# X kept centred in SBUF from the first stage on, the input's mean added back by a product in the last turning

## The chip, the cores and the metric

The kernel runs on one core of a Trainium2 chip. The metric is the device time of one execution in microseconds. Before the change it is 1280.5 us, the median of three runs (1279.04 to 1280.61).

## What is computed

Four residual blocks follow one another on x of shape (2, 2048, 128): time mixing with a channel-mixing gate, a ternary feed-forward net, a state-space scan, a mixture of experts. Each normalises its input and its output over the 128 channels:

```python
def _layernorm(x, axis=-1, eps=1e-05):
    m = jnp.mean(x, axis=axis, keepdims=True)
    v = jnp.var(x, axis=axis, keepdims=True)
    return (x - m) / jnp.sqrt(v + eps)
...
x = L0_attn_x
x = x + _layernorm(_L0_attn_ref(_layernorm(x), ...))   # 1 time mixing, with its own
...                                                    #   two norms and channel mixing
x = x + _layernorm(_L0_ffn_ref(_layernorm(x), ...))    # 2 ternary feed-forward
x = x + _layernorm(_L1_attn_ref(_layernorm(x), ...))   # 3 state-space scan
x = x + _layernorm(_L1_ffn_ref(_layernorm(x), ...))    # 4 mixture of experts
```

The scan of stage 3 runs over 2048 steps for 256 channels and 16 states, `state = dA * state + dBu`, with `y = sum(state * C)`, after a causal convolution of four taps. Stage 4 sends each token to two of eight experts.

Every addend of x is itself the output of a layernorm, so its mean over the channels is zero. The mean of x over the channels is the same in all four blocks: that of the input.

## The kernel before

X lies in SBUF as 128 channels (partitions) by 2 x 2048 tokens, fp32. Work goes in tiles of N = 512 tokens: NT = 4 tiles in time (t), B = 2 rows of the batch (b), so eight tiles of 128x512. A mean over channels is a mean over partitions, so it is made by TensorE: `G.centre` is the matrix I − 1/128, which gives x minus its mean in a PSUM bank, and `G.ones` holds 1/128 throughout, which gives the mean of squares after ScalarE's square. fp32 products of 128x512 appear in the profile as two instructions.

In each block a tile is first centred by such a product (`centre`, `centre_B`, `next_centre_B`, `prep` step 0, `next_stage` step 0), squared by ScalarE out of the bank, averaged by the ones product, turned into 1/sqrt by a logarithm and an exponential on ScalarE, and multiplied from the bank by VectorE.

The program is four functions with a barrier between each: `phase_time_mix` (0 to 150 us), `phase_ffn` (150 to 470), `phase_ssm` (470 to 976), `phase_moe` (976 to 1279). Each engine has its own instruction list, written out by hand in the order of execution; semaphores join them. A wait stands in its engine's list and holds everything behind it.

- `phase_time_mix`: PE's `centre(t)` writes banks C[0], C[1]; `square` and `inverse_roots` are ScalarE's, `normalise` (L615, L616) is VectorE's. At its end the first tile of stage 2 is prepared (`next_centre_B`, L361; `next_square_B`, L504; `next_normalise`, L734). Names: tiles in the order P2_ORDER = (1, 2, 0, 3) in stage 2.
- `phase_ffn`: PE runs through fp16 products in groups; at groups 8 and 13 of each tile stand the centrings of block B for the two rows of the next tile (`centre_B`, L928). At its end L1037 centres the first tile of stage 3.
- `phase_ssm`: tiles 2 to 5 run in a hardware loop over t with two bodies (b = 0, 1), the others are written out. A body has 16 states, n = 0 to 15. For each n VectorE makes `dBu` (L1995) and the scan (L1982), and GpSimd (POOL) multiplies the states by C (`prod`, L1936) and keeps the last column (`keep`, L1929). Besides, the engines prepare the next tile (`prep`): PE at the states in PE_PREP, centring at n = 0 into bank Q[0] (L1582), VectorE at n = 1 with a copy of three columns of halo (L1964) and the normalisation (L1966), `xn = Q[0] * rstd`, on which PE's convolution (L1593) waits. In the last body, `next_stage` prepares six tiles of stage 4: centring, a square, and a copy of the centred bank into `G.normed[i]` (`next_parked`), which POOL multiplies there (`next_normalise`).
- `phase_moe`: routing, then GROUPS = 8 tiles gathered, multiplied and scattered; tiles 6 and 7 are centred at its start (L2214), the others come from stage 3. In the tail each of the eight groups is read back (`back`), added and scaled by VectorE, ScalarE and POOL, turned into the layout of X by four PE products into bank R1 (L2348, 128x128 each), added to X by VectorE (L2753) and stored.

Of the kernel before, what the change touches and what calls it, by code (L numbers as in the profile page):

```python
# [5 lines left out]
F32 = mybir.dt.float32  # L6
# [29 lines left out]
for _name, _count in (  # L36
# [8 lines left out]
SSM_NAMES = ("logA wsum wmean wcentred carry0 centred squared variance logs rstd normed halo conv parked projected gates "  # L45
# [3 lines left out]
         "next_centred next_squared next_parked next_variance next_logs next_rstd next_normed").split()  # L49
# [115 lines left out]
def phase_time_mix(nc, G):  # L165
# [4 lines left out]
    with mem:  # L170
        def sb(name, shape, dt=F32):
# [33 lines left out]
                 "centred2 squared2 variance2 log2 rstd2 scaled2 carried carried_sums "  # L205
                 "h_tsg h_mixed h_keys h_relus h_squares h_gate_in h_gate h_values h_gated h_residual "
                 "h_centredA h_squaredA h_varianceA h_logA h_rstdA h_scaledA h_addedA "
                 "h_centredB h_squaredB h_varianceB h_logB h_rstdB h_normedB").split()
# [32 lines left out]
        def _(pe):  # L241
# [64 lines left out]
            def ln2_centre(t, rows=range(B)):  # L306
                for b in rows:
                    pe.wait_ge(S["added"], at(t, b))
                    pe.wait_ge(S["ln1"], at(min(t + 2, NT - 1), b))
                    if t >= NT - 1:  # L310
                        pe.wait_ge(S["scaled2"], at(t - 1, b))
# [47 lines left out]
            def next_centre_B(b):  # L359
                pe.wait_ge(S["h_addedA"], b + 1)  # L360
                nc.tensor.matmul(V[b][:], G.centre, X[:, b, ds(FIRST)], start=True, stop=True).then_inc(S["h_centredB"], 1)  # L361

# [50 lines left out]
        def _(act):  # L413
# [13 lines left out]
            def inverse_roots(t):  # L427
                for b in range(B):
# [11 lines left out]
                    nc.scalar.activation(rstd[:, b, :], lnv[:, b, :], ACT.Exp, scale=-0.5).then_inc(S["rstd"], 1)  # L440

# [60 lines left out]
            def next_square(b, ready, done):  # L502
                act.wait_ge(ready, b + 1)
                nc.scalar.activation(hsq[:, b, :], V[b][:], ACT.Square).then_inc(done, 1)  # L504
# [7 lines left out]
            def next_square_B(b):  # L512
                next_square(b, S["h_centredB"], S["h_squaredB"])
# [5 lines left out]
            inverse_roots(0)  # L519
            square(1)  # L520
# [37 lines left out]
            for b in range(B):  # L558
                next_square(b, S["h_centredA"], S["h_squaredA"])
# [22 lines left out]
        def _(dve):  # L582
# [149 lines left out]
            def next_normalise(b):  # L732
                dve.wait_ge(S["h_rstdB"], b + 1)
                nc.vector.scalar_tensor_tensor(out=hz[:, b, :], in0=V[b][:], scalar=WS, in1=hsq[:, b, :],  # L734
# [46 lines left out]
def phase_ffn(nc, G):  # L781
# [9 lines left out]
    with mem:  # L791
        def sb(name, shape, dt=F32):
# [47 lines left out]
                 "centredB squaredB varianceB logB rstdB normedB z_high z_low "  # L840
# [45 lines left out]
        def _(pe):  # L886
# [39 lines left out]
            def centre_B(t, b):  # L926
# [1897 lines left out]
```

## Time and profile before

| | us |
|---|---|
| median of three runs | 1280.5 |
| profiled execution | 1280.58 |
| its span | 1278.8 |
| PE busy | 1082.7 (85%) |
| PE weight loads busy | 547.4 (43%) |
| DVE busy | 955.2 (75%) |
| ACT busy | 748.4 (59%) |
| POOL busy | 730.6 (57%) |

The span is one execution from the first instruction to the last; 1.8 us lie around it. PE is TensorE's matmuls, DVE is VectorE, ACT is ScalarE, POOL is GpSimd. The granted clock of TensorE is a number between 0.5 (1.2 GHz) and 1 (2.4 GHz); its mean over the span is 0.946. The shares are averages over four stages with different limits, so the windows by stage, below, say more. In rows of the timeline the columns are start in us, duration in us, engine, line, operation, output and inputs, shapes, and in brackets the idle time before it with what ended it.

### The profile page before, as it was taken

How to read it: one execution, taken by the hardware profiler on the slowest of the kernel's cores; microseconds unless marked ns; L12 is line 12 of the kernel's file. 1: busy time of each engine (PE TensorE's matmuls, PEld its weight loads, DVE VectorE, ACT ScalarE, POOL GpSimd, SP SyncE). 2: the span in 40 equal slices, each digit the busy share in tenths (PEclk: the TensorE clock that was granted, in tenths of full speed). 3: DMA queues.
4: the chain of work that ended last, by engine and by line, in shares of the span. 5: the costliest groups of instructions: out<-in, count | busy, mean ns of one | idle time of the engine just before them, and what ended most of it. 6: DMA issues, size and time to landing. Idle time of an engine off the chain costs nothing. (4 is left out here: it accounts for less than half of the span.)

```text
span 1278.8 us, 16507 instructions
## 1 busy us (share of the span) xinstructions
PE 1082.7 (85%) x4934; PEld 547.4 (43%) x4934; DVE 955.2 (75%) x1181; ACT 748.4 (59%) x1306; POOL 730.6 (57%) x640
## 2 busy tenths in 40 slices
PE   7876799999999987888989898989898388887853
PEld 3322244444444433333334333333335277776753
DVE  4898585665755439999999999999991876565545
ACT  6586545655556255767767686857653345454445
POOL 0222261431513005899898989897983167777764
PEclk8898899999999998999999999999998589999986
DMA  7000000000000003222322222222210111111225
GB/s 232 1 0 0 1 1 1 1 1 1 1 1 1 1 0 109 100 83 93 98 84 88 86 84 92 70 69 77 73 58 9 58 36 50 51 54 51 50 58 182
DMA packets 33966, 67.21 MB, mean 53 GB/s; under 512 B 7168, under 2 KB 7360, under 8 KB 33664
## 3 DMA queue, kind: packets, MB, share of 16 engines
q1 hardware_dynamic: 28464, 55.23, 13.4%
q0 software_dynamic: 4992, 10.23, 3.0%
q8 instruction: 42, 0.69, 0.2%
q10 hardware_dynamic: 432, 0.76, 0.2%
q14 instruction: 36, 0.29, 0.1%
HBM read 56.63 MB, written 9.57 MB: 52 GB/s over the span
## 5 line engine op out<-in xcount | busy, mean ns | idle before, releaser
L1936 POOL TENSOR_TENSOR prod<-hs,csb 128x1024 f32<-128x1024 f32 x128 | 301.9, 2359 | 125.3 <-DVE hs L1982 120.0
L1982 DVE TENSOR_TENSOR_SCAN hs<-dA,first,pD 128x1024 f32<-128x1024 f32 x128 | 300.4, 2347 | 5.2 <-DVE pD L1995 0.8
L1664 PE MATMUL pY<-prod,const 128*128 128x512 f32 x512 | 241.5, 597 | 5.0 <-POOL prod L1936 5.0
L1809 ACT ACTIVATE dA<-dt,negA 128x511 f32<-128x511 f32 x256 | 169.4, 712 | 1.5 <-DVE dt L2037 1.4
L1995 DVE TENSOR_TENSOR pD<-dtu,pD 128x1024 f32<-128x1024 f32 x128 | 154.9, 1211 | 10.0 <-ACT pD L1824 9.7
L1664 PEld LDWEIGHTS pY<-prod,const 128*128 128x128 f32 x512 | 97.5, 192 | 109.9 <-issue 92.2
L2471 POOL DMA_INDIRECT g<-moe_rows,source x78 | 82.4, 1056 | 55.5 <-DVE source L2666 26.7
L2717 DVE SCALAR_TENSOR_TENSOR hid<-pR,silu 128x512 f32<-128x512 f32 x78 | 53.9, 692 | 67.2 <-ACT silu L2425 67.2
L1162 ACT ACTIVATE stage<-pR,vec 128x512 f32<-128x512 f32 x64 | 43.9, 687 | 99.7 <-PE pR L891 99.5
L2490 POOL DMA_INDIRECT moe_outs<-y,to x78 | 81.1, 1039 | 26.2 <-issue 22.8
L1824 ACT ACTIVATE pD<-first 128x1 f32<-128x1 f32 x128 | 21.6, 169 | 119.4 <-PE pD L1674 98.2
L2425 ACT ACTIVATE silu<-pR 128x512 f32<-128x512 f32 x78 | 46.6, 597 | 73.9 <-PE pR L2210 73.9
L2208 PE MATMUL pR<-x,moe_hi 128*128 128x256 f16 x312 | 85.8, 275 | 1.2 <-DVE x L2701 1.2
L2210 PE MATMUL pR<-x,moe_lo 128*128 128x256 f16 x312 | 85.7, 275 | 0.0
L2209 PE MATMUL pR<-x,moe_hi 128*128 128x256 f16 x312 | 85.7, 275 | 0.0
L576 POOL TENSOR_TENSOR o<-o,rs 128x512 f32<-128x512 f32 x8 | 14.0, 1744 | 110.0 <-DVE o L692 110.0
L1674 PE MATMUL pD<-split,sel 96*128 96x512 bf16 x128 | 50.3, 393 | 28.4 <-DVE hs L1982 28.2
L1593 PE MATMUL pQ<-xn,convw 128*128 128x512 f32 x112 | 59.3, 656 | 15.0 <-DVE xn L1966 15.0
L1200 POOL TENSOR_TENSOR K_lo<-kstage,K_hi 128x512 f16<-128x512 f32 x24 | 29.1, 1217 | 52.0 <-DVE K_hi L1267 52.0
L1206 POOL TENSOR_TENSOR A_lo<-stage,A_hi 128x512 f16<-128x512 f32 x32 | 43.0, 1348 | 27.5 <-DVE A_hi L1341 27.5
L2320 PE MATMUL pY<-moe_hi,hid_hi 128*128 x312 | 56.4, 219 | 0.8 <-DVE hid_lo L2708 0.8
L2322 PE MATMUL pY<-moe_hi,hid_lo 128*128 x312 | 56.2, 219 | 0.0
(477 smaller groups left out, 2588.1 us busy)
## 6 DMA issues: line engine op xcount, KB each, us to landing
csb<-ssm_c SPq DMA_DIRECT2D x128, 256.0 KB, 3.1
raw<-moe_w SPq DMA_DIRECT2D x12, 512.0 KB, 4.8
room<-moe_outs SPq DMA_DIRECT2D x8, 512.0 KB, 8.3
hidw<-hid_w SPq DMA_DIRECT2D x1, 2048.0 KB, 10.0
moe_rows<-xt SPq DMA_DIRECT2D x8, 256.0 KB, 2.0
outT<-X SPq DMA_DIRECT2D x8, 256.0 KB, 2.0
X<-xT SPq DMA_DIRECT2D x3, 512.0 KB, 4.1
g<-moe_rows,source POOLq DMA_INDIRECT x78, 2.6
```

The lines of the kernel that those rows point to most:

```text
L1593: last = nc.tensor.matmul(Q[c][:], convw[:, c, k, :], xn[b][:, k:k + N], start=k == 0, stop=k == TAPS - 1)
L1664: last = nc.tensor.matmul(YB[c][:], G.ident, prod[:, slot(b, n), c, :], start=n == 0, stop=n == DST - 1)
L1809: last = nc.scalar.activation(dA[:, slot(b, n), c, 1:N], dt[:, b, c, 1:N], ACT.Exp, scale=negA[:, c, n:n + 1])
L1936: nc.gpsimd.tensor_tensor(prod[:, slot(b, n), :, :], hs[:, slot(b, n), :, :], csb[:, slot(b, n), :, :].to_broadcast([P, CB, N]), ALU.mult)\
L1982: nc.vector.tensor_tensor_scan(hs[:, slot(b, n), :, :].rearrange("p c n -> p (c n)"), dA[:, slot(b, n), :, :].rearrange("p c n -> p (c n)" ...
L1995: nc.vector.tensor_tensor(both_dBu(n), dtu[:, b, :, :], bcastB(n).unsqueeze(1).to_broadcast([P, CB, N]), ALU.mult)\
L2208: nc.tensor.matmul(out, w_hi, x_hi, start=start, stop=False)
L2209: nc.tensor.matmul(out, w_hi, x_lo, start=False, stop=False)
L2210: return nc.tensor.matmul(out, w_lo, x_hi, start=False, stop=stop)
L2320: nc.tensor.matmul(out, hid_hi[:, n % HR, at], w_hi, start=u == 0 and h == 0 and r == 0, stop=False)
L2471: nc.gpsimd.indirect_dma_start(g[:, i % GR, r, :], None, rows, bass.IndirectOffsetOnAxis(ap=source[:, 2 * i + r:2 * i + r + 1], axis=0))\
L2490: nc.gpsimd.indirect_dma_start(outs, bass.IndirectOffsetOnAxis(ap=to[:, 2 * i + r:2 * i + r + 1], axis=0), y[:, i % YR, r, :], None).then_ ...
```

## The change

X is overwritten by its centred copy in stage 1 and stays centred. Stages 2 to 4 take it as it is, without a centring product. The mean of the input has to be put back into the output: the input is loaded a second time in stage 4, and a product of `ones` with it opens each bank of the last turning.

```diff
 phase_time_mix
+            def keep_centred(t):
+                for b in range(B):
+                    act.wait_ge(S["ln1"], at(t, b))
+                    nc.scalar.activation(X[:, b, ds(t)], C[b][:], ACT.Copy).then_inc(S["x_centred"], 1)
...
             inverse_roots(0)
+            keep_centred(0)
...
                 log_of_sums(t)
+                if t + 1 < NT:
+                    keep_centred(t + 1)
...
 PE, centre(t) and ln2_centre(t)
+                        pe.wait_ge(S["x_centred"], at(t - 1, b))
...
-            next_centre_B(0)
...
-            next_centre_B(1)
...
 phase_ffn
-            def centre_B(t, b):
-                pe.wait_ge(S["addedA"], ahead(t, b))
-                nc.tensor.matmul(M[b][:], G.centre, X[:, b, tile(t)], start=True, stop=True).then_inc(S["centredB"], 1)
...
-            nc.tensor.matmul(R[0][:], G.centre, X[:, 0, 0:N], start=True, stop=True).then_inc(G.ssm["centred"], 1)
...
-                square(b, M[b], S["squaredB"], S["centredB"], ahead(t, b))
+                square(b, X[:, b, tile(t)], S["squaredB"], S["addedA"], ahead(t, b))
...
 phase_ssm, PE
-                if step == 0:
+                if step == 1:
+                    pe.wait_ge(S["squared"], at(t, b))
                     wait_past(pe, S["relu"], chunk(t, b, 0) - 1)
-                    wait_past(pe, S["scaledC"], at(t, b) - 3)
-                    nc.tensor.matmul(Q[0][:], G.centre, X[:, b, ds(t)], start=True, stop=True)\
-                      .then_inc(S["centred"], 1)
...
 phase_ssm, ScalarE
-                    act.wait_ge(S["centred"], at(t, b))
-                    nc.scalar.activation(sq[:, b, :], Q[0][:], ACT.Square).then_inc(S["squared"], 1)
+                    wait_past(act, S["scaledC"], at(t, b) - 3)
+                    wait_past(act, S["split3"], at(t, b) - B)
+                    wait_past(act, S["c_out"], 16 * (at(t, b) - B))
+                    wait_past(act, S["b_out"], 16 * (at(t, b) - B))
+                    nc.scalar.activation(sq[:, b, :], X[:, b, ds(t)], ACT.Square).then_inc(S["squared"], 1)
...
-                    nc.scalar.activation(sq[:, i % 2, :], Q[0][:], ACT.Square).then_inc(S["next_squared"], 1)
-                    nc.scalar.activation(G.normed[i], Q[0][:], ACT.Copy).then_inc(S["next_parked"], 1)
+                    nc.scalar.activation(sq[:, i % 2, :], X[:, i % B, i // B * N:(i // B + 1) * N], ACT.Square)\
+                      .then_inc(S["next_squared"], 1)
...
 phase_ssm, GpSimd
-                nc.gpsimd.tensor_tensor(G.normed[i], G.normed[i], sq[:, i % 2, :], ALU.mult).then_inc(S["next_normed"], 1)
+                nc.gpsimd.tensor_tensor(G.normed[i], X[:, i % B, i // B * N:(i // B + 1) * N], sq[:, i % 2, :], ALU.mult)\
+                  .then_inc(S["next_normed"], 1)
...
 phase_ssm, VectorE
-                nc.vector.tensor_tensor(xn[b][:, TAPS - 1:], Q[0][:], rstd[:, b, :], ALU.mult)\
+                nc.vector.tensor_tensor(xn[b][:, TAPS - 1:], X[:, b, ds(t)], rstd[:, b, :], ALU.mult)\
                   .then_inc(S["normed"], 1)
...
 phase_moe
+        again_0 = sb("again4", [P, GROUPS // 2, N])
...
+            def rows_again(i):
+                b, t = tile_of(i)
+                sp.dma_start(again[i], G.xT[:, b, t]).then_inc(S[f"x_again{i // (GROUPS // 2)}"], 16)
+
+            for i in range(GROUPS // 2):
+                rows_again(i)
...
+            sp.wait_ge(S["down"], UNITS)
+            for i in range(GROUPS // 2, GROUPS):
+                rows_again(i)
...
-            centre(EARLY)
-            centre(EARLY + 1)
...
+            pe.wait_ge(S["silus"], UNITS)
             for i in range(GROUPS):
-                pe.wait_ge(S["scaledC"], i + 1)
                 if i >= 2:
                     pe.wait_ge(S["addedC"], i - 1)
+                pe.wait_ge(S[f"x_again{i // (GROUPS // 2)}"], 16 * (GROUPS // 2))
+                nc.tensor.matmul(R1[:, i % 2, :], G.ones, again[i], start=True, stop=False)
+                pe.wait_ge(S["scaledC"], i + 1)
                 for j in range(TC):
                     last = nc.tensor.matmul(R1[:, i % 2, j * P:(j + 1) * P], scaled[:, i % 2, j * P:(j + 1) * P], G.ident,
-                                            start=True, stop=True)
+                                            start=False, stop=j == TC - 1)
```

The same replacement of the bank by X stands in the products of block B (L1288), of the hand-over (L1398) and of stage 4. The second four loads go into `hid_hi` and `hid_lo`, which are free when the experts are done.

On TensorE in stage 2, in the first tile, between the last products of the hidden layer (bank pR) and the channel-mixing values (bank pY), there stood before:

```order
L889 MATMUL pR_2<-hidw,hid_hi 128x512
L890 MATMUL pR_2<-hidw,hid_hi 128x512
L891 MATMUL pR_2<-hidw,hid_lo 128x512
L928 MATMUL pM_0<-X,const 128x512
L889 MATMUL pY_1<-K_hi,cv_hi 128x512
L890 MATMUL pY_1<-K_lo,cv_hi 128x512
L891 MATMUL pY_1<-K_hi,cv_lo 128x512
```

and there stands now:

```order
L893 MATMUL pR_2<-hidw,hid_hi 128x512
L894 MATMUL pR_2<-hidw,hid_hi 128x512
L895 MATMUL pR_2<-hidw,hid_lo 128x512
L893 MATMUL pY_1<-K_hi,cv_hi 128x512
L894 MATMUL pY_1<-K_lo,cv_hi 128x512
L895 MATMUL pY_1<-K_hi,cv_lo 128x512
```

The centring product is gone, and nothing has moved into its place; it is so at six places.

On VectorE in stage 3, in the first body of the hardware loop, at n = 1, the scan, the halo copy, the normalisation and the next `dBu` with their waits stood like this before:

```order
L1982 SCALAR_TENSOR_TENSOR hs<-dA,first,pD 128x1024 [waits ssm_kept,ssm_prod]
L1962 REGISTER_ALU
L1964 COPY xn_1<-xn_1 128x3 [waits ssm_rstd]
L1966 TENSOR_TENSOR xn_1<-pQ_0,sq 128x512 [waits ssm_halo]
L1991 REGISTER_ALU
L1995 TENSOR_TENSOR pD<-dtu,pD 128x1024 [waits ssm_scan,ssm_spliced]
```

and stand like this now:

```order
L1974 SCALAR_TENSOR_TENSOR hs<-dA,first,pD 128x1024 [waits ssm_kept,ssm_prod]
L1954 REGISTER_ALU
L1956 COPY xn_1<-xn_1 128x3 [waits ssm_rstd]
L1958 ISA [waits ssm_halo]
L1958 TENSOR_TENSOR xn_1<-X,sq 128x512
L1983 REGISTER_ALU
L1987 TENSOR_TENSOR pD<-dtu,pD 128x1024 [waits ssm_scan,ssm_spliced]
```

The tile of X depends on the loop's register, so an address calculation stands ahead of the product and has its wait. In the bodies outside the loop there is none. `sq` is the buffer that holds rstd.

At the end of TensorE's list, behind the last product of the experts, there stood before:

```order
L2322 MATMUL pY<-moe_hi,hid_lo 128x128
L2348 MATMUL pR_4<-const,sq 128x128 x32
L2074 UNCONDITIONAL_BRANCH
```

and the end of the list is now:

```order
L2346 MATMUL pR_4<-hid_hi,const 128x512
L2349 MATMUL pR_4<-const,sq 128x128 x4
L2346 MATMUL pR_4<-hid_lo,const 128x512
L2349 MATMUL pR_4<-const,sq 128x128 x4
L2346 MATMUL pR_4<-hid_lo,const 128x512
L2349 MATMUL pR_4<-const,sq 128x128 x4
L2066 UNCONDITIONAL_BRANCH
```

A product of 128x512 with the reloaded input comes ahead of each four turnings, eight times in all.

## Rows read from the trace of the kernel before

**Rows 1.** Busy time by windows: window, length, busy per engine, clock, DMA, GB/s.
```profile
0.00:150.00 150.00, 112.97 (x223) 44.33 (x224) 111.66 (x179) 94.89 (x132) 26.91 (x20) 0.90 0.15 50
150.00:470.00 320.00, 312.43 (x1302) 138.17 (x1302) 191.73 (x332) 170.66 (x231) 87.32 (x68) 0.99 0.00 1
470.00:976.00 506.00, 443.14 (x1051) 177.82 (x1051) 466.85 (x298) 342.27 (x636) 428.08 (x353) 0.97 0.25 80
...
1243.00:1279.00 36.00, 12.51 (x64) 10.76 (x64) 18.15 (x96) 16.12 (x80) 15.27 (x32) 0.64 0.50 176
```
**Rows 2.** The page's costliest groups, those of VectorE in stage 3.
```profile
L1982 DVE TENSOR_TENSOR_SCAN hs<-dA,first,pD 128x1024 f32<-128x1024 f32 x128 | 300.4, 2347 | 5.2 <-DVE pD L1995 0.8
...
L1995 DVE TENSOR_TENSOR pD<-dtu,pD 128x1024 f32<-128x1024 f32 x128 | 154.9, 1211 | 10.0 <-ACT pD L1824 9.7
```
**Rows 3.** Groups by line and shape, TensorE, the centrings of block B.
```profile
L928 PE MATMUL pM<-X,const 128*128 128x512 f32 x12 | 6.1, 592 | 0.0
```
**Rows 4.** Timeline of TensorE at the end of stage 2.
```profile
453.80 1.02 PE L1037 MATMUL pR<-X,const 128*128 128x512 f32 x2
454.66 1.88 PE L1040 MATMUL pR<-stage,const 128*128 128x512 f32 x4
```
**Rows 5.** Timeline at the start of stage 1.
```profile
11.34 1.06 ACT L440 ACTIVATE rstd<-lnv 128x1024 f32<-128x1024 f32 x1
...
11.75 4.16 PE L256 MATMUL pC<-X,const 128*128 128x512 f32 x4 [2.57 <-DVE G L616]
```
**Rows 6.** Timeline at the end of stage 1.
```profile
136.58 1.26 POOL L578 TENSOR_TENSOR XA<-o,xn 128x512 f32<-128x512 f32 x1
...
136.86 1.53 DVE L729 TENSOR_TENSOR X<-X,xn 128x512 f32<-128x512 f32 x1
...
139.61 0.60 ACT L504 ACTIVATE hsq<-pV 128x512 f32<-128x512 f32 x1 [0.46 <-PE pV L361]
139.91 0.69 DVE L729 TENSOR_TENSOR X<-X,xn 128x512 f32<-128x512 f32 x1
```
**Rows 7.** Timeline of stage 3 at n = 1, in the second body and the fourth.
```profile
553.41 2.36 POOL L1936 TENSOR_TENSOR prod<-hs,csb 128x1024 f32<-128x1024 f32 x1 [0.19 <-DVE hs L1982]
553.42 0.69 DVE L1966 TENSOR_TENSOR xn<-pQ,sq 128x512 f32<-128x512 f32 x1
...
670.32 1.08 DVE L1964 COPY xn<-xn 128x3 f32<-128x3 f32 x1
671.31 0.19 POOL L1929 COPY carry<-hs 128x2 f32<-128x2 f32 x1
671.43 0.69 DVE L1966 TENSOR_TENSOR xn<-pQ,sq 128x512 f32<-128x512 f32 x1
671.45 2.36 POOL L1936 TENSOR_TENSOR prod<-hs,csb 128x1024 f32<-128x1024 f32 x1
...
672.18 2.42 PE L1593 MATMUL pQ<-xn,convw 128*128 128x512 f32 x4 [2.07 <-DVE xn L1966]
```
**Rows 8.** Groups by line, VectorE in stage 3, its shortest instruction.
```profile
L2045 DVE MEMSET dtu<- 128x1 f32 x1 | 0.1, 59 | 0.1
```
**Rows 9.** Timeline of VectorE at n = 8 of the fourth and the fifth body.
```profile
695.26 1.23 DVE L1995 TENSOR_TENSOR pD<-dtu,pD 128x1024 f32<-128x1024 f32 x1 [1.68 <-ACT pD L1824]
...
754.20 1.23 DVE L1995 TENSOR_TENSOR pD<-dtu,pD 128x1024 f32<-128x1024 f32 x1 [0.39 <-ACT pD L1824]
```
**Rows 10.** Windows again: a piece of stage 3 just behind that gap.
```profile
674.00:676.00 2.00, 2.00 (x4) 0.99 (x3) 2.00 (x2) 0.93 (x3) 0.27 (x1) 0.50 0.31 107
```
**Rows 11.** Timeline of TensorE at the start of stage 4.
```profile
976.37 2.77 PE L2214 MATMUL pR<-X,const 128*128 128x512 f32 x4 [2.55 <-PEq L162]
```
**Rows 12.** Timeline of the tail.
```profile
1260.97 1.16 PE L2348 MATMUL pR<-const,sq 128*128 128x128 f32 x8 [0.25 <-POOL sq L2504]
1260.99 0.68 DVE L2753 TENSOR_TENSOR X<-X,pR 128x512 f32<-128x512 f32 x1
...
1263.27 0.68 DVE L2753 TENSOR_TENSOR X<-X,pR 128x512 f32<-128x512 f32 x1
```

More of the change, by code:

```diff
@@ L42 @@
     NV += _count
-SSM_NAMES = ("logA wsum wmean wcentred carry0 centred squared variance logs rstd normed halo conv parked projected gates "
+SSM_NAMES = ("logA wsum wmean wcentred carry0 squared variance logs rstd normed halo conv parked projected gates "
          "h xproj ts_in split1 whole rest1 split2 split3 dt_in magnitude expm log1p relu "
@@ L500, in next_gate, with next_square @@
                 nc.scalar.activation(hrc[:, b, :], R[b][:], ACT.Sigmoid).then_inc(S["h_gate"], 1)
-            def next_square(b, ready, done):
+            def next_square(b, src, ready, done):
                 act.wait_ge(ready, b + 1)
-                nc.scalar.activation(hsq[:, b, :], V[b][:], ACT.Square).then_inc(done, 1)
+                nc.scalar.activation(hsq[:, b, :], src, ACT.Square).then_inc(done, 1)
             def next_inverse_root(b, variance, log, done):
@@ L1172, in _ @@
                 square_C(NT - 1, b)
-            act.wait_ge(G.ssm["centred"], 1)
-            nc.scalar.activation(z[:, 0, :], R[0][:], ACT.Square).then_inc(G.ssm["squared"], 1)
+            act.wait_ge(S["addedC"], at(P2_ORDER.index(0), 0))
+            nc.scalar.activation(z[:, 0, :], X[:, 0, 0:N], ACT.Square).then_inc(G.ssm["squared"], 1)
             act.wait_ge(G.ssm["variance"], 1)
@@ L1287, in normalise_B @@
             def normalise_B(t, b):
-                scale(b, M[b], S["rstdB"], S["normedB"], ahead(t, b), z[:, b, :])
+                scale(b, X[:, b, tile(t)], S["rstdB"], S["normedB"], ahead(t, b), z[:, b, :])
             def z_high(t, b):
@@ L1637, in tail @@
             def tail(t, b, step):
-                if is_final(t):
-                    pe.wait_ge((S["next_parked"], S["next_logs"])[step], EARLY)
+                if is_final(t) and step == 1:
+                    pe.wait_ge(S["next_logs"], EARLY)
                 if step == 0:
@@ L2152, in phase_moe @@
         total = hid[:, :, :].rearrange("p r (j d) -> p r j d", j=TC)
+        again_0 = sb("again4", [P, GROUPS // 2, N])
+        spent = [w[:, :, :].rearrange("p r s -> p (r s)").bitcast(F32) for w in (hid_hi, hid_lo)]
+        again = [again_0[:, i, :] for i in range(GROUPS // 2)] + [w[:, k * N:(k + 1) * N] for w in spent for k in range(2)]
         sums = sb("sums4", [P, CHUNKS])
@@ L2167, in phase_moe @@
         names = ("lanes lanes_in consts "
-                 "centred squared variance logs rstd normed xn_high xn_low scores turned rows_out rows_out2 rows_in0 rows_in1 "
+                 "squared variance logs rstd normed xn_high xn_low scores turned rows_out rows_out2 rows_in0 rows_in1 "
                  "logits best1 equal1 code1 first1 picks1 masked best2 equal2 code2 first2 picks2 gap ratio logs2 share squared_share "
@@ L2210, in product @@
                 return nc.tensor.matmul(out, w_lo, x_hi, start=False, stop=stop)
-            def centre(i):
-                b, t = tile_of(i)
-                nc.tensor.matmul(R1[:, i % 2, :], G.centre, X[:, b, t], start=True, stop=True).then_inc(S["centred"], 1)
             def variance(i):
@@ L2354, in square @@
             def square(i):
-                act.wait_ge(S["centred"], late(i) + 1)
-                nc.scalar.activation(sq[:, i % 2, :], R1[:, i % 2, :], ACT.Square).then_inc(S["squared"], 1)
+                b, t = tile_of(i)
+                nc.scalar.activation(sq[:, i % 2, :], X[:, b, t], ACT.Square).then_inc(S["squared"], 1)
             def inverse_root(i):
```

54 lines of the change are left out of this document (22 added, 32 removed).

## The prediction

> **What bounds the kernel now.** I read the busy time of each engine in the four stages first [rows 1]. Columns are window, length, busy time of PE, weight loads, DVE, ACT and POOL, granted clock, DMA. Stage 2 (150 to 470 us) is TensorE's: 312.4 of 320 us busy, at clock 0.99. Stage 3 (470 to 976) is VectorE's: 466.9 of 506 us, with POOL at 428.1 and PE at 443.1. The last 36 us, the tail, are a pipeline over groups in which nobody is full and TensorE's clock is 0.64 on average.
>
> The grouped lines say what stage 3 is made of [rows 2]: DVE alternates a scan of 2347 ns and a product of 1211 ns, 128 times each, and waits 15 us in all before them. POOL's product (2.36 us [rows 7]) runs beside each scan. So a microsecond more on DVE in stage 3 is a microsecond more of the kernel, and a microsecond less on PE there is worth nothing by itself. In stage 2 it is the other way round.
>
> The change takes centring products off PE (cheap to judge) and turns inputs of ACT, DVE and POOL from a PSUM bank into X in SBUF (the risk).
>
> **Stage 2, removed products.** Six fp32 centring products go [rows 3]: 12 instructions, no idle time before them. What one costs PE is read from a back-to-back pair: L1037 starts at 453.80 and the next product at 454.66, 0.86 us [rows 4]. Six are 5.16 us. PE is the full engine there, and what waited for the product (the square of block B) reads X and becomes ready earlier, so nothing new is late. Bounds: 0 if PE's time turned into waiting, 5.16 if none does; I take 5.16 since the stage leaves PE only 7.6 us of idle time.
>
> **Hand-over to stage 3.** L1037 goes too. The two spreads of the skip weights, L1040, and then the variance product queue behind it on PE, so the chain to the first normalised tile moves up by 0.86 us.
>
> **Stage 1.** ACT makes eight copies of 128x512 of the centred bank, about 0.60 us each (the square L504 of that shape and source took 0.60 [rows 6]). Six of them fall into the loop, where ACT has gaps (94.9 of 150 us busy [rows 1]); they cost nothing as long as these last. The first two stand on a chain: PE's centring of tile 1 into the same banks began at 11.75 after DVE's last read [rows 5]; now it must wait for ACT's copy, and ACT's exp ends only at 11.34 + 1.06 = 12.40. Row 0 of the batch can start at about 12.40 + 0.60 + 0.15 = 13.15, 1.4 us later, row 1 hardly later. I take +1.0 (bounds +0.3, where the stage's later gaps absorb it, and +2.5, where TensorE's low clock there lasts longer). At the end of the stage the centring of X for the hand-over (two products) goes; the square L504 waited 0.46 us for one, and ACT is the busy engine of that piece: 0.5 us saved (0 to 1.5).
>
> **Stage 4, its start.** The two centrings L2214 stand first on PE, 2.77 us with clock low [rows 11], but the gate products behind them wait for DVE's lanes nearly as long: −0.4 us (bounds −1 and +1).
>
> **The tail.** The mean of the input comes back as a product of ones with the reloaded input, one per group of eight, in the bank before the four turnings. It costs 0.86 us at full clock [rows 4], a turning of four took 1.16 [rows 12]. Together 2.02, under DVE's period of 2.28 us per group (its additions L2753 start at 1260.99 and 1263.27 [rows 12]). It can run before the scaled rows are ready, so what remains is the part that isn't hidden: the second group's, whose bank and PE's turn come together (about 0.65), and 0.25 at the last. +0.9 us. Bounds 0 and +9 (all eight at 1.2 GHz: 2 x 2.02 = 4.0 against 2.28 is 1.8 a group, over five groups). The eight loads are 1 MB before and 1 MB behind loads that the tail already has; the first half is long there, the second lands behind the `back` loads while the first groups run; no cost, with the bound inside the +9.
>
> Sum so far: −5.16 −0.86 −0.5 +1.0 −0.4 +0.9 = −5.0 us. Without stage 3's change of operands the kernel would take 1275.6.
>
> **Stage 3, the decisive edit.** Thirteen products leave PE and six copies leave ACT there, neither the bound. But VectorE's normalisation L1966 (0.69 us, seven times) had one input in PSUM and one in SBUF; as L1958 it has both in SBUF. Does that matter? The trace has such an instruction beside POOL: at 136.86 X<-X,xn took 1.53 us while POOL's product ran from 136.58 to 137.84; the same line alone at 139.91 took 0.69 [rows 6]. It ended 0.55 after POOL's did, so it was held until POOL had nearly finished. POOL's own 1.26 stayed what it is elsewhere. With an input in PSUM there is no such hold: at 671.43 the normalisation took 0.69 beside a POOL product from 671.45 that took its usual 2.36 [rows 7].
>
> So all depends on which of the two starts first. If DVE is first, POOL is held for 0.7 us, which it can afford. If POOL is first, DVE is held for the whole product. Before, DVE started 0.02 us ahead in this body (671.43 against 671.45); of the seven places the two stand within 0.02 us of each other in six, and in the first DVE is well ahead. They meet because both leave the same event: POOL's preceding product ends, the held copy L1964 (1.08 us for three columns) ends with it at 671.40, POOL does its small copy L1929 (0.19), and both go on. The instruction order says what is new: in the four bodies of the loop (tiles 2 to 5) an address calculation now stands between the copy and the normalisation, and takes over its wait. What it costs no row shows; the nearest is the shortest DVE instruction, a memset at 59 ns [rows 8]; bounds 0 and 0.19 (the small copy L1929 [rows 7]). I take 0.06: DVE comes out 0.04 behind POOL in four bodies, and stays as it is in the three others (there I count none lost, though in one of them POOL is ahead by 0.01: 553.41 against 553.42 [rows 7]).
>
> Price: 2.36 − 0.07 = 2.29 us of DVE per body, four times, 9.2 us. Bounds per body: −0 (DVE first) and 2.36. Nothing takes it back: the scan queued behind it is the bound, and DVE's only wait later in the body (before L1995, for ACT's splice) hangs on the same chain through PE's convolution and shifts with it.
>
> A second term hangs on it. PE waits 2.07 us for the normalisation before its convolution L1593 [rows 7]; now 4.4. In two of the four loop bodies the clock already fell to 0.50 after that gap [rows 10], and the splice came late: DVE waited 1.68 us at 695.26, against 0.39 at 754.20 in a body where it didn't fall [rows 9]. The difference, about 1.3, I count for the two bodies of the loop that had kept their clock: +2.4. Bounds 0 and +6, where the longer gap makes each fall longer.
>
> Stage 3: +9.2 + 2.4 = +11.6. Total: −5.0 + 11.6 = +6.5 us, on 1280.58 us for the profiled execution (span 1278.8 and 1.8 around it), 0.1 above the median: **1287.0 us**.
>
> On the hold, the Trainium skill (SBUF — State Buffer, "Who interferes with whom") says that a DVE instruction with two SBUF inputs contends with a GpSimd instruction that reads SBUF, and "Issue order, not op shape, decides who blocks". The row at 136.86 bears it out by 0.84 us. A sharing of the port instead would stretch the 0.69 to about twice, 0.7 us a body, 2.8 in all, and the total would be about 1278.5; by the rule it is the 1287 above. On the clock the skill (TensorE: Matmul & The Clock Gate, "HAM oscillation — how this bites in real kernels") says that long idle gaps of PE throttle it again. In this trace 2.07 us were on the edge, twice enough and twice not in the loop; by the rule 4.4 us gives the full +2.4, without it the sum is 1284.6.
>
> **Rivals.**
> First, VectorE stays first (the address calculation is hidden behind the wait, or POOL's own start has a margin that the records don't show). Then POOL is held for 0.7 us in each body, with waits of its own to absorb it (428 of 506 busy), DVE loses nothing, and the sum is −5.0 plus 0 to 0.5 of second effects: 1275.8, faster. For it: the margin is 0.02 us in the records, no more than their own grain. Against it: DVE had no reserve either, and every new instruction falls on its side.
> Second, the order flips in one or two bodies only: 2.3 to 3.6 each, total 1278 to 1282, most of it within 0.2%.
> Third, slower still: the bodies outside the loop go as well (six lost, 13.7 us) and three clocks fall (+3.9): 1280.6 − 5.0 + 17.6 = 1293. For it: POOL is ahead in one such body already.
> Fourth, the ones products run at 1.2 GHz in the tail, whose mean clock is 0.64: TensorE then takes 4.0 us a group instead of DVE's 2.28, +3 to +9 on top of either. Against it: the products themselves keep PE busy.
> Fifth, stage 2 gives nothing back since another wait ends there: 5.2 more. Against it PE's 98% there.
>
> **Chances.** Forecast 0.50 (own range 1283 to 1290), VectorE first 0.27, one or two bodies 0.12, six bodies 0.06, tail at the low clock or stage 2 without gain 0.05 together, counted as slower. This measurement can tell 0.2%, 2.6 us. Faster than 1277.9: 0.27. Between: 0.12. Slower than 1283.1: 0.61. The range runs from the first rival to the third: 1275.5 to 1293.5.
>
> **What would show it.** The profile after should have the normalisation L1958 at 2.9 to 3.1 us in four of seven places (0.69 if VectorE was first, and then POOL's L1936 beside it at about 3 us); DVE busy in stage 3 up by 9 us; PE's longest waits for it at 4.4 us and the clock at 0.50 behind them; stage 2 shorter by 5.2 us and still full; tail 1 us longer, with additions of X at 2.3 us. I am wrong if L1958 keeps 0.69 everywhere, or if stage 2 isn't 5 us shorter.

## The result, and the profile after

The changed kernel takes 1289.2 us (median of four runs, 1288.16 to 1291.71) against 1280.0 for the one before (four runs): ratio 1.0076, 95% interval 1.0063 to 1.0088. The forecast was 1287.0. It is slower by about the amount forecast, but not by the steps forecast; the experiments below are about that.

The profiled execution took 1288.16 us, span 1286.3. Its busy times by windows, as in [rows 1], the tail's window shifted by 7 us:

```profile
0.00:150.00 150.00, 112.44 (x218) 44.33 (x218) 111.42 (x175) 99.11 (x140) 26.93 (x20) 0.89 0.15 50
150.00:470.00 320.00, 310.83 (x1293) 136.78 (x1294) 193.76 (x344) 172.47 (x234) 87.29 (x68) 0.99 0.00 1
470.00:976.00 506.00, 432.49 (x1004) 173.75 (x1003) 472.23 (x286) 335.10 (x624) 427.09 (x352) 0.96 0.25 80
...
1250.00:1286.00 36.00, 16.57 (x78) 11.41 (x78) 18.26 (x96) 16.12 (x80) 15.28 (x32) 0.74 0.58 207
```

The windows are cut at the times of the kernel before. Stage 3 now begins about 6 us earlier and ends about 7 us later, so its last piece lies behind the third window (VectorE has 286 instructions there for 298). VectorE is busier in it all the same (472.2 us for 466.9), although stage 3 gives it the same instructions. TensorE does more in the tail, whose clock is higher (0.74 for 0.64).

Where the time went is seen by setting the 128 scans of stage 3 beside each other, execution against execution. The first scan starts 5.88 us earlier than before (480.93 for 486.81), the last 7.44 us later (963.75 for 956.31), and the last addition to X in stage 4 ends 7.52 us later. So stages 1 and 2 with the hand-over gave 5.9 us, stage 3 cost 13.3, stage 4 nothing in this pair of executions. How far one execution can be trusted is seen from the runs below that have the same code in a stage: their first scans start between 479.37 and 482.61 us, and their stage 4, from the last scan to the end of the last addition, takes 317.2 to 323.8 us. Stage 3's cost is well above such differences; a microsecond in stage 4 is not. Within stage 3 the loss stands at one place: between the scans of states 1 and 2, in the six bodies that have a halo copy (the second to the seventh), each of them 2.4 to 2.6 us longer than before. The grouped lines of VectorE and of TensorE's variance product, before:

```profile
L1587 PE MATMUL pQ<-sq,const 128*128 128x512 f32 x14 | 7.3, 600 | 2.5 <-ACT sq L1729 2.5
L1966 DVE TENSOR_TENSOR xn<-pQ,sq 128x512 f32<-128x512 f32 x7 | 4.8, 688 | 0.2
L1964 DVE COPY xn<-xn 128x3 f32<-128x3 f32 x6 | 4.3, 718 | 0.0
```

and after:

```profile
L1579 PE MATMUL pQ<-sq,const 128*128 128x512 f32 x14 | 11.7, 933 | 3.2 <-ACT sq L1718 3.2
L1956 DVE COPY xn<-xn 128x3 f32<-128x3 f32 x6 | 11.6, 1939 | 6.8 <-ACT sq L1710 6.8
L1958 DVE TENSOR_TENSOR xn<-X,sq 128x512 f32<-128x512 f32 x7 | 4.8, 689 | 0.7 <-DVE xn L1956 0.3
```

The normalisation, on which the forecast put the loss, is as short as before (689 ns against 688). The copy of three columns ahead of it is what grew: 11.6 us for 4.3, and 6.8 us of waiting before it for 1/sigma. That is 14.1 us in these two numbers. The variance product takes 933 ns per instruction instead of 600.

The timeline of the fourth body, where [rows 7] stood, tells the order of things. TensorE, ScalarE, POOL and VectorE after:

```profile
663.34 0.39 PE L1660 MATMUL pD<-split,sel 96*128 96x512 bf16 x1 [0.39 <-DVE hs L1974]
665.30 0.61 ACT L1718 ACTIVATE sq<-X 128x512 f32 x1
666.13 2.48 PE L1650 MATMUL pY<-prod,const 128*128 128x512 f32 x4 [2.40 <-POOL prod L1928]
668.40 1.92 PE L1579 MATMUL pQ<-sq,const 128*128 128x512 f32 x2
671.59 0.63 ACT L1710 ACTIVATE sq<-sq 128x512 f32<-128x512 f32 x1
672.24 2.35 POOL L1928 TENSOR_TENSOR prod<-hs,csb 128x1024 f32<-128x1024 f32 x1
672.25 2.36 DVE L1956 COPY xn<-xn 128x3 f32<-128x3 f32 x1 [1.05 <-ACT sq L1710]
674.76 0.69 DVE L1958 TENSOR_TENSOR xn<-X,sq 128x512 f32<-128x512 f32 x1
675.50 1.98 PE L1586 MATMUL pQ<-xn,convw 128*128 128x512 f32 x4 [2.90 <-DVE xn L1958]
```

and the same links before:

```profile
663.23 1.12 PE L1582 MATMUL pQ<-X,const 128*128 x2 [1.06 <-DVE scaled L1973]
665.33 1.98 PE L1664 MATMUL pY<-prod,const 128*128 128x512 f32 x4 [0.77 <-POOL prod L1936]
667.15 1.02 PE L1587 MATMUL pQ<-sq,const 128*128 128x512 f32 x2
669.24 0.63 ACT L1724 ACTIVATE sq<-sq 128x512 f32<-128x512 f32 x1
```

Before, the centring product cut TensorE's gap at a body's start in two, 1.06 and 0.77 us. After, it is one gap of 2.40 us, and the windows show the clock behind it: 1.00 before, 0.50 after, in the same two microseconds.

```profile
668.00:670.00 2.00, 2.00 (x6) 0.76 (x4) 1.97 (x2) 1.54 (x4) 2.00 (x2) 1.00 0.33 113
```
```profile
668.00:670.00 2.00, 2.00 (x3) 0.49 (x2) 1.96 (x2) 0.00 (x0) 2.00 (x4) 0.50 0.27 73
```

At 1.2 GHz the variance product takes 1.92 us instead of 1.02, and 1/sigma is ready 6.88 us after the body's first scan began (665.34) instead of 5.32 (664.55). The scan of state 1 ends at 5.85. So 1/sigma used to be there when VectorE came for it, and now VectorE waits 1.05 us. In that microsecond POOL finishes one product and begins the next, at 672.24. The halo copy comes at 672.25, 0.01 us behind it, and stands for 2.36 us, until POOL's product ends. Before, it was issued while POOL's preceding product still ran (to 671.37), and was held only for what was left of that: it took 1.08 us in all.

### The profile page after: what moved, and what is told of

Its sections match the earlier page's. It is cut to its first block and busy times, and to the rows that moved or that the text cites. A ratio compares the mean times of both kernels' runs of the same rounds, so it can differ in the third digit from the quotient of the medians.

```text
span 1286.3 us, 16479 instructions
## 1 busy us (share of the span) xinstructions
PE 1076.4 (84%) x4902; PEld 542.7 (42%) x4902; DVE 963.6 (75%) x1181; ACT 749.0 (58%) x1308; POOL 732.2 (57%) x640
## 5 line engine op out<-in xcount | busy, mean ns | idle before, releaser
L1650 PE MATMUL pY<-prod,const 128*128 128x512 f32 x512 | 248.2, 611 | 14.6 <-POOL prod L1928 14.6
```

Source lines behind the costliest of these rows:

```text
L1650: last = nc.tensor.matmul(YB[c][:], G.ident, prod[:, slot(b, n), c, :], start=n == 0, stop=n == DST - 1)
```

## Experiments

Theory A: without the centring product TensorE's clock falls at a body's start, 1/sigma comes late, and the copy lands behind POOL's next product. Theory B is the one of the forecast: the normalisation with both inputs in SBUF is itself held when POOL starts first. All ratios are against runs of the kernel before on the same chip, with a 95% interval.

**e1_filler.** The centring product back on TensorE, its result unused:

```diff
+            def filler(t, b):
+                wait_past(pe, S["relu"], chunk(t, b, 0) - 1)
+                wait_past(pe, S["scaledC"], at(t, b) - 3)
+                nc.tensor.matmul(Q[0][:], G.centre, X[:, b, ds(t)], start=True, stop=True)
...
+                    if not is_last(t, b) and n == 0:
+                        filler(*after(t, b))
```

> The changed kernel, but TensorE keeps one product of the centring matrix with the next tile of X at the place in each scan-stage body where the centring stood; its result is read by nobody. Theory A (clock): without that product TensorE idles 2.4 us at a body's start, its clock falls to 0.50, the variance product takes 1.9 instead of 1.0 us and 1/sigma reaches VectorE about 2 us late, behind the start of POOL's next product, which then holds the halo copy for 2.3 us. By A the variance products take 600 ns per instruction again (933 in the changed kernel), the copy starts at the scan's end. Theory B (the one on record: the normalisation with both inputs in SBUF is held by POOL's product in the loop bodies, where an address calculation lets POOL go first). If A alone matters: 1275 us, 14 less than the changed kernel. If B matters too once the copy is early again: 1284 to 1287, with the normalisation at about 3 us in four bodies. If A is wrong: 1289, as the changed kernel.

Measured: 1302.1 us, ratio 1.0154 (1.013 to 1.0177), dearer than either theory had it. Yet A's own links came out as it says: the variance product takes 599 ns again, the copy 0.14 to 1.12 us as before, without a wait. And now the normalisation is hit, in all six bodies that have a copy. The fourth and the last of them:

```profile
671.87 1.09 DVE L1963 COPY xn<-xn 128x3 f32<-128x3 f32 x1
673.01 2.34 POOL L1935 TENSOR_TENSOR prod<-hs,csb 128x1024 f32<-128x1024 f32 x1
673.10 2.80 DVE L1965 TENSOR_TENSOR xn<-X,sq 128x512 f32<-128x512 f32 x1
...
675.95 2.93 PE L1586 MATMUL pQ<-xn,convw 128*128 128x512 f32 x3 [4.29 <-DVE xn L1965]
```
```profile
862.93 2.37 POOL L1935 TENSOR_TENSOR prod<-hs,csb 128x1024 f32<-128x1024 f32 x1
862.94 2.91 DVE L1965 TENSOR_TENSOR xn<-X,sq 128x512 f32<-128x512 f32 x1
```

This is theory B as the forecast had it, down to TensorE's wait of 4.3 us (4.4 expected) and the fall of the clock behind it. In the four loop bodies VectorE comes 0.09 to 0.11 us behind POOL, in the two outside the loop, without the address calculation, 0.01 and 0.02 us behind: that is enough. Both theories are true, and the second was masked in the changed kernel, because there the copy had already been held past POOL's product. The two mishaps exclude each other in one body, and the masked one is the dearer: 20.9 us in stage 3 instead of 13.3. The six holds add 13.3 us between the scans of states 1 and 2; the rest comes later in the body, where TensorE's clock falls under the convolutions and VectorE's waits before its products grow from 10.0 to 16.7 us. Of the 14 us between the profiled executions of this run and the changed kernel 7.6 lie in stage 3, the rest in stage 4, whose code is the same.

**e2_old_prep.** The stage's preparation with the bank again:

```diff
+                if step == 0:
+                    ...
+                    nc.tensor.matmul(Q[0][:], G.centre, X[:, b, ds(t)], start=True, stop=True)\
+                      .then_inc(S["centred"], 1)
...
-                    nc.scalar.activation(sq[:, b, :], X[:, b, ds(t)], ACT.Square).then_inc(S["squared"], 1)
+                    nc.scalar.activation(sq[:, b, :], Q[0][:], ACT.Square).then_inc(S["squared"], 1)
...
-                nc.vector.tensor_tensor(xn[b][:, TAPS - 1:], X[:, b, ds(t)], rstd[:, b, :], ALU.mult)\
+                nc.vector.tensor_tensor(xn[b][:, TAPS - 1:], Q[0][:], rstd[:, b, :], ALU.mult)\
```

> The changed kernel with the scan stage's preparation of a tile as in the kernel before: the centring product into the bank, ScalarE's square and VectorE's normalisation read the bank (the rest of the change stays: X centred, no centring in the feed-forward stage, none for the next stage, the ones products of the tail). Theory A and B both expect 1274 to 1275 us, 6 less than before, since both put the loss into the preparation; they part from e1_filler: A expects no difference between the two, B 9 us or more. A third theory, that the loss is in another edit of the scan stage (POOL's product out of X, the missing copies), expects over 1280.

Measured: 1275.4 us, ratio 0.9962 (0.9948 to 0.9976). The rest of the change is worth about what the forecast gave it (4.7 us; 5.0 forecast, without stage 3). From e1_filler it differs in where the square and the normalisation read, and in the waits ahead of the square. The times are 26.7 us apart; 21.2 of it lie between the first and the last scan, and most of the rest in stage 4, where the two have the same instructions. So 21 us are the price of normalising from SBUF here, nearly all of it in the six bodies with a copy.

**e3_copy_early.** The copy one state earlier, ahead of the wait for 1/sigma:

```diff
                 dve.wait_ge(S["rstd"], at(t, b))
                 if not is_start(t):
-                    nc.vector.tensor_copy(xn[b][:, 0:TAPS - 1], xn[b][:, N:N + TAPS - 1]).then_inc(S["halo"], 1)
                     dve.wait_ge(S["halo"], at(t, b) - B)
...
+                    if n == 0 and not is_last(t, b) and not is_start(after(t, b)[0]):
+                        halo(*after(t, b))
```

> The changed kernel with VectorE's halo copy of three columns one state earlier, behind the first scan of a body, ahead of the wait for 1/sigma; the clock's fall stays as it is. It asks what the held copy costs, and whether the normalisation itself, both inputs in SBUF, is held when POOL's product is already running. If only the copy is ever held: the wait of 1.05 us for 1/sigma stays, the 2.3 us hold goes (the early copy may be held for up to 1 us): 1289 less 6 x 1.3, about 1281. If the normalisation is held as well (theory B's mechanism): it is at 2.9 us in its place and the time stays at 1288 to 1290.

Measured: 1282.0 us, ratio 1.0012 (0.9993 to 1.0031), between the two cases. In three of six bodies the normalisation was held in the copy's place, in one for 0.9 us, in two hardly at all (0.73 and 0.76 us). In these two the clock had not fallen and 1/sigma was early, against the expectation, so that the normalisation was issued before POOL's next product. One body of each kind:

```profile
727.94 2.35 POOL L1928 TENSOR_TENSOR prod<-hs,csb 128x1024 f32<-128x1024 f32 x1
728.10 2.74 DVE L1961 TENSOR_TENSOR xn<-X,sq 128x512 f32<-128x512 f32 x1 [0.32 <-ACT sq L1710]
```
```profile
668.78 0.76 DVE L1961 TENSOR_TENSOR xn<-X,sq 128x512 f32<-128x512 f32 x1
668.94 0.65 POOL L1921 COPY carry<-hs 128x2 f32<-128x2 f32 x1
```

There POOL was the one held: behind the second of these its small copy took 0.65 us for 0.19, in the other body its product 2.69 for 2.35. So the order of issue decides, per body.

The body that kept its clock had a gap on TensorE as long as the fourth body of the changed kernel:

```profile
662.95 1.98 PE L1650 MATMUL pY<-prod,const 128*128 128x512 f32 x4 [2.39 <-POOL prod L1928]
```

The four products behind it took 1.98 us, at full clock, where the changed kernel's took 2.48 and fell on the way. So without the centring product the clock may fall at a body's start, but need not, and these runs do not show what decides it.

**e4_no_mean.** No second load of the input and no products with ones in the tail (the output lacks the input's mean):

```diff
-                nc.tensor.matmul(R1[:, i % 2, :], G.ones, again[i], start=True, stop=False)
```

> The changed kernel without the second load of the input and without the eight products with ones in the tail: the output lacks the input's mean. The forecast priced them at +0.9 us, so 1288.3 against 1289.2; the trace of the changed kernel puts the tail at the length of the one before (its last turnings ran at full clock, those before at half), so without the products the clock should be low in the last three turnings and the time the same within 0.5 us.

Measured: 1289.6 us, ratio 1.0066 (1.004 to 1.0091), the same as the changed kernel as far as five runs can tell. Against the changed kernel's trace its last scan is 3.74 us later and its last addition 3.16 (1283.42 for 1280.26): stage 4 is 0.6 us shorter without the products, less than it differs between runs of one code. They keep the clock up for the last turnings, as expected; the eighth turning of the changed kernel and the sixth of this one:

```profile
1279.16 1.05 PE L2349 MATMUL pR<-const,sq 128*128 128x128 f32 x8
```
```profile
1278.23 1.97 PE L2342 MATMUL pR<-const,sq 128*128 128x128 f32 x8 [0.85 <-POOL sq L2498]
```

Its stage 3 has the code of the changed kernel, yet in the fourth and the fifth body the clock was kept and the other mishap came, in the same execution as the held copies of the others:

```profile
671.98 2.34 POOL L1928 TENSOR_TENSOR prod<-hs,csb 128x1024 f32<-128x1024 f32 x1
672.07 2.80 DVE L1958 TENSOR_TENSOR xn<-X,sq 128x512 f32<-128x512 f32 x1
```

These two bodies took 2.7 and 1.3 us longer than in the changed kernel's trace. They are where the later last scan comes from, and not the edit.

**e5_pool_norm and e6_pool_norm_filler.** With X in SBUF both inputs of the normalisation lie there, and it is given to POOL, whose other products also read SBUF; the halo copy goes to ScalarE. e6 has the filler as well.

```diff
 ScalarE
+            def halo(t, b):
+                act.wait_ge(S["projected"], chunk(t, b, CB - 1) - B * CB)
+                nc.scalar.activation(xn[b][:, 0:TAPS - 1], xn[b][:, N:N + TAPS - 1], ACT.Copy).then_inc(S["halo"], 1)
...
+                    if n == 0 and not is_last(t, b) and not is_start(after(t, b)[0]):
+                        halo(*after(t, b))
...
 GpSimd, behind the product of state 1
+            def normalise(t, b):
+                pool.wait_ge(S["rstd"], at(t, b))
...
+                nc.gpsimd.tensor_tensor(xn[b][:, TAPS - 1:], X[:, b, ds(t)], rstd[:, b, :], ALU.mult)\
+                  .then_inc(S["normed"], 1)
...
+                    if not is_last(t, b) and n == 1:
+                        normalise(*after(t, b))
...
 VectorE
-                    if not is_last(t, b) and n == DVE_PREP:
-                        prep(*after(t, b))
```

> The changed kernel with the normalisation of the scan stage on POOL (X times 1/sigma, both in SBUF, behind POOL's product of state 1) and the halo copy on ScalarE (behind its square at state 0): VectorE issues nothing there that needs the port pair which POOL uses, and 0.6 us less work per tile. TensorE has no filler, so its clock falls as in the changed kernel and 1/sigma comes about 2 us late; POOL waits for it and TensorE's convolution starts 1 to 1.5 us later than before. If the loss of 13 us in the scan stage was VectorE being held (2.5 us in six bodies) and nothing else, it goes entirely and some 4 us of the old copies with it: 1268 to 1273. If instead the late 1/sigma itself costs time through TensorE and ScalarE: 1277 or more.

> As e5_pool_norm, with the unread centring product on TensorE at state 0 that keeps its clock: 1/sigma is early again. Against e1_filler (1302 us) only the engine of the normalisation and of the halo copy differ; if the port hold is its whole loss it falls by some 30 us to 1268 to 1272. Against e5_pool_norm it tells what the clock's fall costs when VectorE can't be held: 0 to 3 us if little, more if TensorE's late start matters.

Measured: 1308.9 us (1.0218, 1.0194 to 1.0243) and 1312.4 us (1.0246, 1.0222 to 1.027). Both are far above the times expected; e5 lies in its second case (1277 or more), but by 30 us and by a cause that I had not named. VectorE was held nowhere, yet the place was wrong: POOL runs a product behind VectorE, so "behind the product of state 1" is one state late. From e6:

```profile
682.42 1.30 POOL L1939 TENSOR_TENSOR xn<-X,sq 128x512 f32<-128x512 f32 x1
...
683.77 1.22 PE L1586 MATMUL pQ<-xn,convw 128*128 128x512 f32 x1 [5.10 <-POOL xn L1939]
```
```profile
L2003 DVE TENSOR_TENSOR pD<-dtu,pD 128x1024 f32<-128x1024 f32 x128 | 155.0, 1211 | 50.2 <-ACT pD L1823 50.2
```

TensorE waited 5.1 us for xn, the splices behind it (ScalarE's `pD<-first`, which writes a column into the bank that VectorE multiplies next) came late, and VectorE waited 50.2 us for them (10.0 before [rows 2]). So the time at which xn is ready has a price of its own on the path.

**e8_pool_norm_first and e9_pool_norm_first_nofiller.** The same two with `n == 0` for `n == 1` on POOL.

> e6_pool_norm_filler (1312 us) with POOL's normalisation one state earlier in its list, behind the product of state 0. There it stood behind the product of state 1, xn was ready at 683.7 in a body that began at 673, TensorE idled 5.1 us and the splice of later states came late (VectorE waited 50 us in all for it). Now it can run as soon as 1/sigma is there: xn about 1.2 us later than VectorE's in the kernel before. If only the place was wrong: 1268 to 1274, no more than e7_halo_act's 1268.9 by much. If POOL's later products matter: 1278 or more.

> The same without the filler (e5_pool_norm with the earlier place): the whole of the change's idea, no centring product in the scan stage at all, and VectorE free of the port. The clock falls at a body's start, 1/sigma comes about 2 us late. If VectorE's hold is all that this costs: 1268 to 1275. If the late 1/sigma costs through TensorE's late convolution and the splices: 1280 or more, some 2 us per body above e8_pool_norm_first.

Measured: 1283.9 us (1.0039, 1.002 to 1.0058) and 1278.8 us (1.0002, 0.9982 to 1.0021). The place was most of it, 28 and 30 us. But e8 came out 10 us over its first case and lies in its second (1278 or more), and e9 lies between its two: VectorE still waits 23.6 us for splices in e8, 17.4 in e9. The traces say where they part. In the last four bodies with a copy the clock under e8's convolutions is 0.59 to 0.69 and VectorE waits 2.3 to 3.0 us before its product of state 3; in e9 the clock there is 1.00 in every body and that wait 0.8 to 1.7. Why the clock was kept in e9 even where TensorE's gap before the convolution was the same (2.67 to 2.69 us in both) stays open. e9 has the whole of the change, the fall of the clock included (in three of six bodies; its variance products take 782 ns on average), and no hold of VectorE: it is 10.4 us under the changed kernel, of which 4.3 (seven times 0.61) are work taken from VectorE.

**e7_halo_act.** e2_old_prep with the halo copy on ScalarE, as above:

> e2_old_prep (1275.4 us: centring product and bank kept in the scan stage) with the halo copy on ScalarE instead of VectorE. The copy took 0.14 to 1.09 us on VectorE in the kernel before, 4.3 us in six bodies, most of it held by POOL's product; the normalisation, with one input in PSUM, can't be held. So 4.3 us less, 1271, and up to 2.6 us less still where TensorE's gap before the convolution gets too short for its clock to fall: 1268.5 to 1271.5. If copies were hidden anyway: 1275.

Measured: 1268.9 us, ratio 0.9905 (0.9881 to 0.9928), in the expected range and the fastest of all. The normalisation, with one input in a bank, is issued at the scan's end and runs beside POOL's product unhindered:

```profile
663.31 2.37 POOL L1934 TENSOR_TENSOR prod<-hs,csb 128x1024 f32<-128x1024 f32 x1
664.61 0.67 DVE L1963 TENSOR_TENSOR xn<-pQ,sq 128x512 f32<-128x512 f32 x1
...
665.32 1.98 PE L1589 MATMUL pQ<-xn,convw 128*128 128x512 f32 x4 [0.93 <-DVE xn L1963]
```

TensorE waits 0.93 us instead of the 2.07 of [rows 7], and the stalls at state 8 [rows 9] go too.

**e10_filler_halo_act.** e1_filler with the halo copy on ScalarE.

> e1_filler (1302 us: filler on TensorE, VectorE normalises from X in SBUF) with the halo copy on ScalarE. Without the held copy ahead of it the normalisation is issued right behind the scan, while POOL's product of state 0 still runs, so it is held for its remaining 0 to 1 us instead of for the whole of the next product (2.8 us in e1_filler, six times). If the hold is exclusive and goes by issue order: normalisations at 0.7 to 1.7 us, 1271 to 1275. If being behind a running product costs a whole product more: as e1_filler, 1296 to 1302.

Measured: 1275.9 us, ratio 0.9968 (0.9954 to 0.9983), 1 us over its first case. It is 26 us under e1_filler (24 by the ratios, 22.2 within stage 3), by moving a copy of three columns. The normalisation still has both inputs in SBUF and is held, but by the rest of a product that is already running:

```profile
662.58 2.36 POOL L1941 TENSOR_TENSOR prod<-hs,csb 128x1024 f32<-128x1024 f32 x1
663.87 1.61 DVE L1970 TENSOR_TENSOR xn<-X,sq 128x512 f32<-128x512 f32 x1
```

In e1_filler the held copy ended together with POOL's product, and so let the normalisation out just when POOL started anew. Against e7_halo_act, with the same products on TensorE and the copy on ScalarE in both, the input in SBUF instead of the bank costs 7.1 us by the medians, and 7.1 within stage 3.

## Why the forecast came out right, and where it was wrong

**Stages 1 and 2: right.** The forecast's terms up to the first scan add to −5.5 us; measured −5.88 (−4.2 to −7.4 by the traces of the experiments, against the one trace of before). By pieces: in stage 1 TensorE's second centring started at 13.37 instead of 11.75 and the first scan there 0.97 us later (+1.0 forecast); its end was +0.29 (149.77 to 150.06; +0.5 forecast). Stage 2 with the hand-over gave 6.17 us (6.02 forecast).

**Stage 4: its start right, its tail not measured finely enough.** The gate products come 0.55 us earlier relative to the last scan (−0.4 forecast). The ones products come out at +0.6 by e4 (+0.9 forecast), and the whole stage at nothing (7.44 to 7.52), but runs with one code in this stage differ by up to 6.6 us, so neither number bears out the forecast's +0.9. What is shown is that the ones products did not cost the +9 of the bound: from the last product of the experts to the last addition it is 36.9 us, for 36.8 before.

**Stage 3: right in sum, wrong in its mechanism.** +13.3 us for a forecast of +11.6. The step that failed is the sentence "Thirteen products leave PE and six copies leave ACT there, neither the bound." It priced the removed centring product by TensorE's busy time alone. Seven of those products also stood in or just ahead of TensorE's gap at each body's start, and without them the clock fell there and 1/sigma came 1.6 to 2.8 us later, past the point at which VectorE asks for it. I had looked at TensorE's gap ahead of the convolution and not at the one that the removal makes.

From this all else followed differently. The forecast's hold of the normalisation (four bodies, 2.29 us each) did not occur in the changed kernel, where L1958 took 0.69 us everywhere: by my own test in the prediction I was wrong there. What was held was the copy ahead of it, in five bodies for 2.2 to 2.4 us, and VectorE waited up to 2.34 us for 1/sigma (in the second body, where no product stood in the way, that wait was the whole loss). In the third body the clock had risen again when the variance product came, but the four products ahead of it had taken 3.68 us at the low clock, for 1.98 before. That both give about 2.4 us per body is no accident of arithmetic, since both are one product of POOL, 2.36 us; but that the number of bodies and the other terms made the same sum is luck. Six bodies were hit, not four: the address calculation was not what decided, as e1_filler shows in the bodies outside the loop. It was small, as I had taken it: between the end of the copy and the normalisation lie 0.14 to 0.16 us in the loop and 0.03 to 0.04 outside, so it costs about 0.12 (0.06 forecast).

The term for the clock, +2.4, had the wrong sign. The long gap in the middle of a body no longer cost what it did: after the change the clock had fallen and risen again before it and was 1.00 under the convolutions in five of the six bodies, and the stalls at state 8 that [rows 9] show at 1.68 us are 0.39 in each of the last four such bodies. With the smaller stalls at state 4 that gave back 3.4 us over the two bodies that had them. In the third body the fall reached under the convolutions and cost 1.7 us more. So stage 3 adds up: +15.1 between the scans of states 1 and 2, +1.7, −3.4, together +13.4 for a measured +13.3.

**The mechanism that I named is real.** e1_filler, e3_copy_early and e10_filler_halo_act show the normalisation held by 2.2, by 2.1 and by up to 1.0 us. The rule of the Trainium skill that the forecast weighed (SBUF — State Buffer, "Who interferes with whom"), that the order of issue decides and the other blocks for the whole instruction, agrees with these rows: a start 0.01 us behind POOL cost a normalisation 2.2 us (2.91 for 0.69). The same section lists `copy` among the operations that can take both ports; the trace agrees, with 0.14 to 2.36 us for the same copy. I had the old copy's 1.08 us before me and did not ask what happens to it when it comes later. The forecast's first rival, VectorE first and POOL held, is real too, though smaller than the 0.7 us it gave: in the first body of stage 3 the normalisation started 0.16 us ahead of POOL's product, and that took 2.71 us, for 2.35 before the change.

## What to carry to other kernels

A product that is taken off an engine which is not the bound may still help to keep that engine's clock up: look at the gap that its removal makes and at what is computed right behind it, not only at busy time. Where VectorE and POOL both run without pause, look at every VectorE instruction whose inputs all lie in SBUF, however small; the time it takes depends on where POOL stands when it is issued, and a copy of three columns could cost 2.4 us or 0.14. Here it paid to give such copies to ScalarE, and to keep one input of the larger product in PSUM even though SBUF had the same data (1268.9 us against 1275.9). And a single trace can mislead: one code showed both mishaps in one execution.

## What the runs showed of the hardware that I had not expected

- A held instruction shows in the trace as busy, not as waiting: the copy of 128x3 stands there with 0.14 to 2.36 us, and raises VectorE's share.
- A VectorE instruction that is held gets in when POOL's product ends, ahead of what POOL issues next: in e1_filler and e10_filler_halo_act POOL's small copy right behind took 0.64 to 0.68 us instead of 0.19.
- A gap of 2.40 us on TensorE put the clock to 0.50 within the products behind it; cut into 1.06 and 0.77 us by one product of 0.86 us it did not. The length of the gap alone does not decide: the clock was kept behind 2.39 us in e3_copy_early and behind 1.93 us in the second body before the change, and fell behind 1.95 us in the same body after it. With a product in the centring's place (before, e1, e2, e6, e7, e8, e10) it fell at the start of one body with a halo copy of 42, without one (the changed kernel, e3, e4, e5, e9) in 20 of 30; what decided in these 30 is not shown.
- A removed loss can uncover a larger one: with the filler the kernel went from 1289 to 1302 us, although the filler did what it was meant to do.
